# Delta-rule stage: two groups of transposing matmuls placed beside other matmuls, on the other half of the PSUM partitions

## What is computed

```python
def step(s, inp):
    qt, kt, vt, at, bt = inp
    s = s * at[..., None]
    u = jnp.einsum('bhd,bhdv->bhv', kt, s)
    s = s + bt[..., None, None] * (kt[..., None] * (vt - u)[..., None, :])
    out = jnp.einsum('bhdv,bhd->bhv', s, qt)
    return (s, out)
```

## Time and profile before

| | |
|---|---|
| median of three runs | 6472.64 us |
| the profiled execution | 6483.2 us |
| its span | 6481.4 us |
| mean granted clock of TensorE | 0.911 of full speed |
| TensorE matmul busy | 5445.0 us, 84% |
| VectorE busy | 3545.8 us, 55% |
| GpSimd busy | 2497.2 us, 39% |
| ScalarE busy | 2313.2 us, 36% |

### The profile page before, as it was taken

One profiled execution on the slowest core, in us unless ns is written; L12 is line 12 of the kernel. 1 busy time (PEld: TensorE's weight loads), 2 busy tenths in 40 slices (PEclk: granted clock), 3 DMA queues, 4 the chain that ended last, 5 costly groups with the idle time before them and its releaser, 6 DMA issues. The chain is left out here.

```text
span 6481.4 us, 183438 instructions
## 1 busy us (share of the span) xinstructions
PE 5445.0 (84%) x72156; PEld 3850.4 (59%) x72156; DVE 3545.8 (55%) x9528; ACT 2313.2 (36%) x4102; POOL 2497.2 (39%) x2792
## 2 busy tenths in 40 slices
PE   4568767888857888888898898987679998997998
PEld 3434344555536777777777777775356665555776
DVE  4532256777775565665565655665345554664343
ACT  3432225666633333333333333333123322011333
POOL 2210013444435666666665666664200000653000
PEclk7779978999978999999998999998789999998999
DMA  0000001000000000000000000000010000000000
GB/s 17 0 18 0 2 0 40 0 0 0 0 1 17 11 11 11 13 11 11 11 13 11 11 11 11 13 11 12 0 40 0 0 0 3 1 1 27 0 0 13
DMA packets 29530, 57.59 MB, mean 9 GB/s; under 512 B 7312, under 2 KB 14240, under 8 KB 28704
## 3 DMA queue, kind: packets, MB, share of 16 engines
q1 hardware_dynamic: 28960, 48.86, 2.4%
HBM read 46.75 MB, written 2.10 MB: 8 GB/s over the span
## 5 line engine op out<-in xcount | busy, mean ns | idle before, releaser
L617 PEld LDWEIGHTS psum<-m_wd,m_h 128*128 128x128 f32 x6144 | 811.4, 194 | 487.3 <-issue 486.2
L617 PE MATMUL psum<-m_wd,m_h 128*128 128x128 f32 x6144 | 824.9, 278 | 92.6 <-remote 63.8
L2077 POOL TENSOR_TENSOR e_kd<-e_kd,e_tail 128x512 f32<-128x512 f32 x325 | 369.2, 1136 | 574.2 <-PE psum L2184 560.7
L607 PE MATMUL psum<-xT,m_wa 128*128 (+1 forms) x1032 | 550.0, 616 | 8.4 <-remote 8.4
L607 PE MATMUL psum<-xT,m_wb 128*128 (+1 forms) x1032 | 539.2, 605 | 0.0
L784 DVE SCALAR_TENSOR_TENSOR m_acc<-psum,m_combine,m_acc 128x128 f32<-128x128 f32 x1440 | 403.6, 342 | 225.1 <-PE psum L617 210.2
L544 POOL TENSOR_TENSOR m_h<-m_td,m_tb 128x512 f32<-128x512 f32 x258 | 329.0, 1275 | 483.7 <-DVE m_tb L812 483.7
L2214 PE MATMUL psum<-e_T,e_N 64*64 64x32 f32 x10400 | 404.6, 231 | 65.2 <-remote 63.9
L2214 PEld LDWEIGHTS psum<-e_T,e_N 64*64 64x64 f32 x10400 | 368.5, 147 | 111.1 <-issue 108.1
L2184 PE MATMUL psum<-e_kd,e_k 64*64 64x64 f32 x10400 | 416.7, 236 | 0.2
L143 POOL TENSOR_SCALAR m_post_rstd<-m_post_mv 128x4 f32<-128x4 f32 x27 | 6.2, 230 | 991.2 <-DVE m_post_mv L133 991.2
(11 more groups left out here) (432 smaller groups left out, 12131.7 us busy)
## 6 DMA issues: line engine op xcount, KB each, us to landing
e_w<-in_e_w SPq DMA_DIRECT2D x66, 321.0 KB, 2.9
m_wa<-in_m_wa SPq DMA_DIRECT2D x12, 512.0 KB, 7.0
m_wd<-in_m_wd SPq DMA_DIRECT2D x12, 512.0 KB, 8.1
m_wb<-in_m_wb SPq DMA_DIRECT2D x8, 512.0 KB, 8.5
f_h<-in_f_h SPq DMA_DIRECT2D x2, 1024.0 KB
out<-x SPq DMA_DIRECT2D x1, 2048.0 KB, 8.7
f_w<-in_f_w SPq DMA_DIRECT2D x3, 256.0 KB
g_w<-in_g_w SPq DMA_DIRECT2D x3, 256.0 KB
```

Of the source, the lines that this page charges most:

```text
L607: pe.matmul(c.ps[i][:], w[q][:, j, :], xb, start=True, stop=True).then_inc(a_ready[i], 1)
L617: r = pe.matmul(c.ps[4 + e % 2][:, t * P:(t + 1) * P], h[:, u % DEPTH, t * P:(t + 1) * P], wd[u // UQ][:, u % UQ, :], start=(m == 0 and t ...
L2077: return g.tensor_tensor(both_odd(dst[:], m), both_odd(src[:], m), gate.unsqueeze(1).broadcast_to((P, 2, nb, m)), ALU.mult)
```

## The change

The turned keys are no longer a call of their own. In `t_step(5)` each chunk's two T matmuls are followed by the chunk's two matmuls on the unit matrix, written to `half(1 - h)` of bank `X_`; so `t_step(5)` waits for `ks_done` too. In the same way `diagonal` and `gram(1)` become `gram_and_diagonal`: after all their waits, each chunk's two Gram matmuls are followed by its two diagonal matmuls, written to `half(1 - h)` of `X_`. As each head's result now lies on the other head's partitions, ScalarE copies `ket` in two instructions of 64 partitions, and VectorE's masked copy of the diagonals becomes two as well (`own_tokens`). The `ket` copies move from the end of ScalarE's turn to the next turn, behind the even columns of `kd`; the odd columns of `k` wait for `ke_ps` in their place. `project_qk`, `square_sums` and `project_gates` are each split into two functions that are called one right after the other.

```diff
-            def diagonal():
-
-                pe.wait_ge(ket_ready, 1)
-                pe.sem_clear(ket_ready)
-                for u in range(NC):
-                    for h in range(2):
-                        r = pe.matmul(c.psum[half(h), X_, chunk(u)], kn[half(h), chunk(u)], kqn[half(h), 1, chunk(u)],
-                                      start=True, stop=True)
-                r.then_inc(d_ps, 1)
...
+            def gram_and_diagonal():
+
+                pe.wait_ge(even_ready, 1)
+                pe.sem_clear(even_ready)
+                pe.wait_ge(lv_ready, 1)
+                pe.sem_clear(lv_ready)
+                pe.wait_ge(gr_free, 1)
+                pe.sem_clear(gr_free)
+                pe.wait_ge(ket_ready, 1)
+                pe.sem_clear(ket_ready)
+                for u in range(NC):
+                    r = gram_chunk(1, k, kd, u)
+                    if u + 1 == NC:
+                        r.then_inc(gr_ps, 1)
+                    for h in range(2):
+                        r = pe.matmul(c.psum[half(1 - h), X_, chunk(u)], kn[half(h), chunk(u)], kqn[half(h), 1, chunk(u)],
+                                      start=True, stop=True)
+                r.then_inc(d_ps, 1)
...
+                if l + 1 == LEVELS:
+                    pe.wait_ge(ks_done, 1)
+                    pe.sem_clear(ks_done)
                 left = (TT0, TT, TT, TT, TTH)[l - 1]
                 for u in range(NC):
                     for h in range(2):
                         r = pe.matmul(even(c.psum[half(h), T_, chunk(u)], 1 << l), left[half(h), chunk(u)], Z[half(h), u, :],
                                       start=False, stop=False, skip_group_check=True)
-                r.then_inc(t_ps, 1)
+                    if u + 1 == NC:
+                        r.then_inc(t_ps, 1)
+                    if l + 1 == LEVELS:
+                        for h in range(2):
+                            r = pe.matmul(c.psum[half(1 - h), X_, chunk(u)], k[half(h), chunk(u)], eye[half(h), :],
+                                          start=True, stop=True)
+                if l + 1 == LEVELS:
+                    r.then_inc(ke_ps, 1)
...
                 cross_t()
-                diagonal()
-                pe.wait_ge(even_ready, 1)
-                pe.sem_clear(even_ready)
-                pe.wait_ge(lv_ready, 1)
-                pe.sem_clear(lv_ready)
-                gram(1, k, kd, gr_free, gr_ps)
+                gram_and_diagonal()
...
                 t_step(5)
-                keys_by_tokens()
...
+            def ket_copies():
+
+                for h in range(2):
+                    r = a.activation(flat(ket[half(h)]), c.psum[half(1 - h), X_, :], ACT.Copy)
+                r.then_inc(ket_ready, 1)
...
                 a.wait_ge(kd_free, 1)
                 a.sem_clear(kd_free)
+                a.wait_ge(ke_ps, 1)
+                a.sem_clear(ke_ps)
                 a.activation(odd(k[:], 1), odd(kn[:], 1), ACT.Copy).then_inc(k_free, 1)
                 a.wait_ge(zx_ps, 1)
                 a.sem_clear(zx_ps)
                 a.activation(flat(ZX), c.ps[Z_][:, 0:TB * CH], ACT.Copy).then_inc(zx_ready, 1)
                 a.activation(both_even(kd[:], 1), both_even(kdn[:], 1), ACT.Copy).then_inc(even_ready, 1)
+                ket_copies()
                 u_copy()
...
                 t_copy(5)
-                a.wait_ge(ke_ps, 1)
-                a.sem_clear(ke_ps)
-                a.activation(flat(ket), c.ps[X_][:], ACT.Copy).then_inc(ket_ready, 1)
...
+            def own_tokens():
+
+                for h in range(2):
+                    r = v.copy_predicated(chunks(AT[half(h)]), eyei[half(h)].unsqueeze(1).broadcast_to((DH, NC, CH)),
+                                          chunks(c.psum[half(1 - h), X_, :]))
+                ch.link(r)
...
-                ch.link(v.copy_predicated(chunks(AT[:]), eyei[:].unsqueeze(1).broadcast_to((P, NC, CH)), chunks(c.ps[X_])))
+                own_tokens()
```

More of the change, by code:

```diff
@@ L2308, in from_state, with project_q @@
                               start=True, stop=False, skip_group_check=True)
-            def project_qk():
+            def project_q():
                 pe.wait_ge(w_ready, 16)
@@ L2315, in project_qk, with project_k, squares_of, sums_q @@
                 pe.sem_clear(hs_ready)
[L2316 to L2320, removed]
+                pe.matmul(c.ps[Q_][:], W[:, 0:P], hs[:], start=True, stop=True)
+            def project_k():
+                pe.matmul(c.ps[K_][:], W[:, P:2 * P], hs[:], start=True, stop=True).then_inc(qk_ps, 1)
+            def squares_of(n):
+                for t in range(TB):
+                    at = 2 * (n * TB + t)
+                    r = pe.matmul(c.ps[X_][:, at:at + 2], sq[:, n, block(t)], hm[:], start=True, stop=True)
+                return r
+            def sums_q():
                 pe.wait_ge(sq_ready, 1)
                 pe.sem_clear(sq_ready)
[L2324 to L2334, removed]
+                squares_of(0)
+            def sums_k():
+                squares_of(1).then_inc(ss_ps, 1)
+            def project_alpha():
+                pe.matmul(c.ps[Q_][:], W[:, 2 * P:3 * P], hs[:], start=True, stop=True)
+            def project_beta():
+                pe.matmul(c.ps[K_][:], W[:, 3 * P:4 * P], hs[:], start=True, stop=True).then_inc(ab_ps, 1)
             def key_norms():
@@ L2370, in output @@
                 r.then_inc(out_ps, 1)
[L2372 to L2383, removed]
+            project_q()
+            project_k()
+            sums_q()
+            sums_k()
+            project_alpha()
+            project_beta()
             key_norms()
@@ L2412, in step @@
                 pe.sem_clear(out_free)
-                project_qk()
+                project_q()
+                project_k()
                 state_and_output(1)
@@ L2416, in step @@
                 z_and_gram(2)
-                square_sums()
+                sums_q()
+                sums_k()
                 t_step(2)
@@ L2420, in step @@
                 z_and_gram(3)
-                project_gates()
+                project_alpha()
+                project_beta()
                 state_and_output(2)
@@ L2439, in _ @@
                     step()
-            for token in (nx_ready, t_ready, tt_ready, ket_ready, kdh_done, kd_ready):
+            for token in (nx_ready, t_ready, tt_ready, kdh_done, kd_ready):
                 pe.wait_ge(token, 1)
@@ L2448, in _ @@
             a.sem_inc(t_ready, 1)
-            a.sem_inc(ket_ready, 1)
+            a.sem_inc(ke_ps, 1)
             a.sem_inc(at_free, 1)
```

## The result

The changed kernel takes 6535.92 us (median of four runs, 6514.48 to 6539.24) against 6472.91 us: a ratio of 1.0097, 95% interval 1.007 to 1.0123. It is 63 us slower. The profiled execution took 6539.24 us, its span is 6537.4 us.

The account below looks back on a forecast made before the run. TensorE looked like the bound (444 of 500 us busy in the delta stage), but waits on GpSimd ended both changed stretches; 65 turns x 0.07 us = +4.5 us gave 6477 us, range 6445 to 6525.

Parts of the forecast that it names:

- the pairs: TensorE's T with keys and Gram with diagonal: each pair of blocks takes 1.00 us instead of 1.91 and 1.94.
- unpaired rival: The pairs don't overlap on TensorE: about 1.9 us a turn more, 6600 us; chance 0.02.
- step 1: Keys beside T: pair waits for GpSimd, starts 0.87 us later, gains 0.04 us; late T takes what the removed `ket` copy gives.
- step 2: Diagonal beside Gram: pair waits for GpSimd, runs 3023.03 to 3024.03, 0.14 us late; about 1.2 us idle after `cross_t`.
- the copies: Second masked copy on VectorE (0.72 us) and second `ket` copy on ScalarE (0.6 us) fall in idle time: nothing.
- From there the list is as before: After the Gram pair, `z_and_gram(1)` starts about 0.06 to 0.08 us late and `solve(0)`'s wait swallows 0.14; nothing else changes.
- clock rival: Idle times where turns meet let TensorE's clock fall every second turn, 1.5 us each: 49 us, 6526 us; chance 0.20.

Follow-up runs that it names:

- The fillers: Matmuls nobody reads, put into the changed kernel's two new idle times; the long ones of `fat_fill` gave 6490.88 us against the changed kernel's 6535.92.
- each half alone: The kernel before with only the T and keys pair (`keys_pair`, 6542.62 us) or only the Gram and diagonal pair (`gram_pair`, 6445.0 us).
- keys_pair: Kernel before plus only the turned keys beside the last T products, `ket` copied by two instructions at its old place: 6542.62 us, ratio 1.0116.
- gram_pair: Kernel before plus only the diagonal beside `gram(1)`, `ket` copied next turn, turned keys a separate block on the other half: 6445.0 us, ratio 0.9973.
- fill_both: Changed kernel with many short unread matmuls, 20 records ahead of the T pair's waits and 32 ahead of the Gram pair's: 6543.44 us, ratio 1.0118.
- thin_before: Kernel before with only the first of the diagonal's 8 chunks computed, leaving TensorE idle there: 6482.26 us, ratio 1.0015.
- fat_fill: Changed kernel with one long unread matmul in each new idle time, 256 columns ahead of the T pair, 448 ahead of the Gram pair: 6490.88 us, ratio 1.0038.
- before_order: Kernel before, nothing paired, with waits reordered in `z_and_gram` and `gram(1)` and VectorE's masked copy ahead of its transpose: 6405.37 us, ratio 0.9883.

## Why the prediction was wrong

**Right: the pairs.** Each takes 0.95 to 0.99 us; I took 1.00. By the rule of the Trainium skill's TensorE: Matmul & The Clock Gate, "Part 3", they would have kept 1.9 us each; the trace of the changed kernel does not agree for alternating quarters of the array, at 0.95 and 0.99 us. The unpaired rival falls.

**Right in its main term: step 1.** The T pair started 0.16 us after GpSimd, as I took it, with an idle time of 0.67 us by the profile (I said 0.9, counted from the old start). The removed `ket` copy was eaten by the late T: the odd `k` came 3095.26 - 3091.31 = 3.95 us after `output`, where it was 3.80 before (`output` then started at 3015.94). I had said 0.01 late, it is 0.15. The T copy came 0.13 earlier than worked out (3.08 us after `output`, not 3.21), but the step from it to the odd `k` took 0.87 us, not 0.6. The profile puts the idle time of 0.49 us before it on the turned keys; they had all started by 3094.08, before even the T copy at 3094.39, so it was hardly they, and what fills the step is not shown.

**Right, but small: step 2.** The Gram pair stood behind GpSimd's product, 0.39 us after it, 0.27 and two more semaphore instructions. Undisturbed turns are 0.23 us longer, not 0.07: 15 us, not 4.5.

**Right: the copies.** VectorE's two masked copies take 1.47 us, and 1.48 us of idle time are still left ahead of the state (2.34 in the earlier trace rows):

```profile
3105.11 1.47 DVE L2610 COPY_PREDICATED e_AT<-e_eyei,psum 64x512 f32<-64x512 int32 x2
3108.05 0.28 DVE L2637 SCALAR_TENSOR_TENSOR e_S<-e_S,e_tH,psum 128x64 f32<-128x64 f32 x1 [1.48 <-PE psum L2302]
```

The Trainium skill's TensorEngine Tiling (Array Packing), "PSUM Bottleneck", says that tiling speeds up TensorE but not the copies out of PSUM. The trace agrees: these copies even doubled, from 0.72 to 1.47 us. Here they were hidden.

**Wrong: "From there the list is as before".** This step took TensorE's two new idle times for free, since the end of the stretch hardly moved. The clock rival had the mechanism, the place and nearly the price (6526 us), and I gave it 0.20, arguing only that this stretch had stayed at full clock before; but it had done so while it was dense. The rival's rate, a fall in every second turn, was what came: 32 turns of 64, where 5 had one before. The mean turn, 64 of them from one copy of the odd `k` to the next, grew from (4444.69 - 1976.28)/64 = 38.57 to (4512.82 - 1979.71)/64 = 39.58 us, 1.01 us; 0.23 is the longer undisturbed turn, and 0.78 (51 us), by subtraction, the falls. The fillers give about 38 us of it back. The range ended at 6525, 11 us short, because it was cut at the clock rival's own value, 49 us over the forecast, which held only 4.5 of the waits' 15 us. The two costs come together, and the sum, 49 + 15 over the median, would have been 6537. That this meets the 6536 so closely is in part luck: the price of 1.5 us for a fall was a guess, and 51 us over 27 more such turns would be 1.9.

What stays open: why each half alone leaves the clock at 0.94 and both together give 0.90 is told by the runs only as far as the place: the two idle times lie within 6 us of each other, and filling the second is enough. The mean hides a part: falls in the first 4 us come in 4 turns of keys_pair and in 13 of gram_pair, but gram_pair has less low time later in the turn (206 us, where the kernel before has 267), which I can't explain. Whether TensorE's stops in fill_both come from the supply of instructions was argued, not shown.

## What to carry to other kernels

Before work is packed closer on the busiest engine, look at what ends last in that stretch: matmuls that fill a wait are free, and taking them away gives nothing and can cost the clock. In either pair one partner is held for the other's late input. That does no harm where nobody waits for the held one soon (the diagonal, read in the middle of the turn) and costs where the chain hangs on it (T, whose copy stands ahead of the odd `k`). And look at the order of a list of waits, with the one that comes last at its end: that, together with a transpose moved out of the way, gave 1.2% here, and at the Gram pair alone nothing.

## What the runs showed of the hardware

Alternating f32 matmuls with 64x64 weights over all four quarters of the array run at twice the rate of two quarters: 64 records in 0.95 to 1.00 us against 32 in 0.95. TensorE's granted clock can fall in a kernel whose TensorE is 82% busy, at the place where work is taken out: with two idle times there it fell in 32 turns of 64, where it had been 5, and one useless matmul of 448 columns a turn brought that back to 5 and made the changed kernel about 38 us faster. thin_before does seven eighths of a block less each turn and is no faster, at 6482 against 6471 us. Many short matmuls are not the same cure: fill_both brought the mean clock back to 0.94 as fat_fill did and was 53 us slower than it, with 46 us of stops inside blocks where fat_fill has 22. Semaphore instructions behind the wait that ends last cost TensorE time: it started 0.15 to 0.16 us after GpSimd's end with one behind the wait (`gram(1)` of before_order, the T pair), 0.27 with three (`gram(1)` before) and 0.39 with five (the Gram pair).
